# Layer 3's product jobs spread over all eight steps of a group, value banks emptied by VectorE, and layer 4's first pair of heads among layer 3's last steps

## What is computed

```python
x = _layernorm(x + _L1_attn_ref(x, Wq, Wk, Wv, Wo, lambda_init))      # layer 3: difference attention
x = _layernorm(x + _L1_xattn_ref(x, ctx_2048, ctx_2048, gamma))       # layer 4: attention over the context
x = _layernorm(x + _L1_ffn_ref(x, ...))                               # layer 5: experts
```

## Time and profile before

| | |
|---|---|
| median of 3 runs | 2112.47 us (2110.99 to 2131.47) |
| profiled execution | 2109.85 us |
| its span | 2107.8 us |
| layer 3's loop and end | about 420 to 754 us of the span |
| layer 4 up to its steady part | about 754 to 783 us |

### The profile page before, as it was taken

The page is one execution under the profiler, slowest core; times in us unless marked ns, Lnnn a source line. Parts: engine busy times, 40 slices in busy tenths (PEclk is TensorE's granted clock), DMA queues, the critical chain, the costliest instruction groups (busy, mean ns, idle before and its releaser), DMA issues.

```text
span 2107.8 us, 30014 instructions
## 1 busy us (share of the span) xinstructions
PE 1858.5 (88%) x11146; PEld 1440.5 (68%) x11160; DVE 1253.2 (59%) x2718; ACT 1014.5 (48%) x2260; POOL 618.5 (29%) x654
## 2 busy tenths in 40 slices
PE   8998898789889779789999979876999788999796
PEld 6885776667777644478888865655888644555585
DVE  3555784466666745544444454685444567888666
ACT  3124784254454447623333322663333369889232
POOL 1212100132232321112222224442222234888322
PEclk9998897899999979889999989986999898999888
DMA  5005402100010110023332310000323101000011
GB/s 211 26 26 120 72 2 93 41 1 7 35 38 1 38 38 1 1 74 123 110 107 98 127 59 1 1 10 31 118 98 102 50 1 38 1 1 1 0 61 41
DMA packets 25622, 105.57 MB, mean 50 GB/s; under 512 B 3642, under 2 KB 9530, under 8 KB 21508
## 3 DMA queue, kind: packets, MB, share of 16 engines
q1 hardware_dynamic: 23316, 101.87, 14.2%
q0 software_dynamic: 1728, 1.58, 0.7%
q10 hardware_dynamic: 432, 0.20, 0.0%
HBM read 97.56 MB, written 6.07 MB: 49 GB/s over the span
## 4 chain that ended last, share of the span: by engine, by line
PE 67%; DVE 14%; ACT 9%; issue 4%; POOL 3%; DMA 2%; SPq 0%; POOLq 0%; DVEq 0%; ACTq 0%
PE ps L145 60%; PE ps L262 6%; ACT AR L148 4%; DVE AR L162 3%; DVE AR L151 2%; DVE Y L151 2%; DVE AR L159 1%; POOL AR L151 1%; DVE stt L325 1%; POOL R L151 1%; DMA AR<-sq 1%; DVE X L156 1%; DVE W L159 1%; POOL rs L151 1%; ACT AR L1680 1%
## 5 line engine op out<-in xcount | busy, mean ns | idle before, releaser
L145 PE MATMUL ps<-R 128*128 128x512 f32 (+3 forms) x4944 | 879.1, 343 | 55.7 <-POOL R L151 33.1
L145 PEld LDWEIGHTS ps<-R 128*128 128x128 f32 (+1 forms) x4944 | 750.4, 194 | 171.9 <-issue 30.9
L151 POOL TENSOR_TENSOR R<-W,R 128x768 fp32r<-128x768 f32 (+2 forms) x106 | 181.5, 1724 | 600.8 <-ACT R L1934 496.0
L148 ACT ACTIVATE AR<-AR 128x128 f32<-128x128 f32 (+4 forms) x585 | 277.4, 549 | 162.0 <-DVE AR L162 106.7
L151 DVE TENSOR_TENSOR AR<-ps,AR 128x512 f32<-128x512 f32 (+5 forms) x266 | 137.5, 536 | 239.8 <-PE ps L145 220.0
L262 PEld LDWEIGHTS ps<-cf,AR 128*128 128x128 f32 (+1 forms) x1168 | 145.8, 148 | 168.2 <-issue 61.0
L262 PE MATMUL ps<-cf,AR 128*128 128x128 f32 (+1 forms) x1168 | 193.6, 290 | 53.2 <-POOL AR L151 14.0
L1960 ACT CAST R<-AR 128x512 fp32r<-128x512 f32 x148 | 92.0, 622 | 304.1 <-DVE AR L151 294.4
L145 PE MATMUL ps<-W,AR 128*128 128x256 f32 (+3 forms) x1200 | 212.3, 353 | 22.1 <-ACT AR L1370 12.5
L145 PE MATMUL ps<-AR 128*32 128x256 f32 (+4 forms) x1600 | 188.0, 337 | 10.3 <-DVE AR L151 7.6
L145 PEld LDWEIGHTS ps<-W,AR 128*128 128x128 f32 (+2 forms) x1200 | 156.9, 164 | 55.0 <-issue 20.5
(11 more groups left out here) (186 smaller groups left out, 2048.2 us busy)
## 6 DMA issues: line engine op xcount, KB each, us to landing
W<-in_wts SPq DMA_DIRECT2D x14, 1920.0 KB, 7.9
AR<-shd SPq DMA_DIRECT2D x32, 512.0 KB, 3.6
W<-in_wts SPq DMA_DIRECT2D x4, 2048.0 KB, 8.5
AR<-shd SPq DMA_DIRECT2D x20, 384.0 KB, 3.4
W<-in_wts SPq DMA_DIRECT2D x5, 1280.0 KB, 7.5
AR<-shd SPq DMA_DIRECT2D x20, 256.0 KB, 3.9
W<-in_wts SPq DMA_DIRECT2D x2, 1536.0 KB, 7.7
AR<-shd SPq DMA_DIRECT2D x20, 128.0 KB, 3.7
```

Source lines behind the costliest of these rows:

```text
L145: return self.e.matmul(o, l, r, start=start, stop=stop, skip_group_check=True)
L148: return self.e.activation(o, i, f, bias=bias, scale=scale)
L151: return self.e.tensor_tensor(o, a, b, op)
```

## The change

In layer 3 the 12 product jobs of the next group are dealt out over all eight steps: 1, 2, 2, 2, 2, 1, 1, 1 jobs in the steps b = 0 to 7. The q and k parts of the weights are split two groups ahead, in step b = 5 of the group before, and the v part in step b = 0. The v banks are copied by DVE. The transposed state is no longer made. Layer 4's first pair moves into layer 3's end: POOL's part into step 60, the scores into step 66, the maxima into 68 and 69, the exponentials into 69; for that its tiles of the first pair lie in the tensor CR. Layer 4's pairs use the score banks 2, 3, 0, 1 in turn. Layer 10's mask is made in layer 5's step 6.

```diff
@@ stage counts
-                N[_l] = Ends(*stage(added=8, aggr=8, rstd=8, normed=8, xturned=8, xt=8))
+                turns = 0 if _l == 3 else 8
+                N[_l] = Ends(*stage(added=8, aggr=8, rstd=8, normed=8, xturned=turns, xt=turns))
@@ need_state_bank
+            elif l == 4:
+                e.wait_ge(*N[3].added.at(8))
@@ DifferenceAttention
-                return job[0] == "v" or (job[0] != "o" and job[2] == 1)
+                return job[0] in ("q", "k") and job[2] == 1
...
                 g, b = divmod(i, 8)
-                return self.products(g + 1)[2 * (b - 1):2 * b] if g < 7 and 1 <= b <= 6 else []
+                first = (0, 1, 3, 5, 7, 9, 10, 11, 12)
+                return self.products(g + 1)[first[b]:first[b + 1]] if g < 7 else []
...
+            @staticmethod
+            def splits(i):
+                g, b = divmod(i, 8)
+                if b == 5 and g < 6:
+                    return [(g + 2, 0), (g + 2, 1)]
+                return [(g + 1, 2)] if b == 0 and g < 7 else []
+
+            def need_split(self, e, g, i):
+                e.wait_ge(*loaded(first_chunk[self.l] + g // 2))
+                if g:
+                    e.wait_ge(*self.T.worked.at(self.place[self.products(g - 1)[7 if i < 2 else 11]] + 1))
... pe
-                    if i >= 63:
+                    if i == 66:
                         e.wait_ge(*T.biased.at(64))
-                        pe_turn_state(e, self.l, i - 63)
-                pe_turn_state(e, self.l, 7)
+                        layers[4].pe_scores(e, 0)
... dve_job
+                    if job[0] == "v":
+                        _, g, t0 = job
+                        e.e.tensor_copy(self.v[g % 2][:, 256 * t0:256 * (t0 + 2)], k).then_inc(T.taken_d.sem, 1)
+                        return
... dve
+                layers[4].dve_parity(e)
...
+                    if i >= 68:
+                        layers[4].dve_max(e, i - 68)
... act
+                for i in range(2):
+                    self.act_split(e, 1, i)
                 for i in range(70):
...
-                        if i % 8 == 0 and i < 56:
-                            self.act_split(e, i // 8 + 1)
+                        for g, part in self.splits(i):
+                            self.act_split(e, g, part)
                     for job in self.jobs(i):
                         self.act_job(e, job)
-                    if i >= 63:
-                        act_copy_state(e, self.l, i - 63)
-                act_copy_state(e, self.l, 7)
+                    if i == 69:
+                        layers[4].act_exps(e, 0)
... pool (the subtractions follow splits(i) in the same way)
+                    if i == 60:
+                        layers[4].pool_front(e)
@@ ColumnAttention
+                early = Room((CR[:, 512:4608].bitcast(F32), 2048), (CR[:, 7168:10368].bitcast(F32), 1600))
+                self.E, self.OS = early.ring(4, 512), room.ring(2, 512)
+                self.KB = [early.take(512), room.take(512)]
+                self.VZ = [early.take(512), room.take(512)]
+                self.OZ, self.par = early.take(64), early.take(2)
+                self.m = early.ring(4, 4)
...
+            def score_bank(i):
+                return banks[(i + 2) % 4]
...
+            def pool_front(self, e):
+                T = self.T
+                e.wait_ge(s_y, 32)
+                e.wait_ge(*T.parity.at(1))
+                self.pool_keys(e, 0)
+                e.e.memset(self.VZ[0], 0.0).then_inc(T.zeroed.sem, 1)
+                e.e.memset(self.OZ, 0.0).then_inc(T.zeroed.sem, 1)
+                e.wait_ge(*T.zeroed.at(2))
+                for h in range(2):
+                    e.e.memset(self.OZ[:, 48 * h:48 * h + 16], 1.0).then_inc(T.ones.sem, 1)
+                e.wait_ge(*T.ones.at(2))
+                self.pool_values(e, 0)
@@ LargeAndSmallExperts, dve_route
+                if j == 6:
+                    layers[10].dve_mask(e)
@@ vector engine
-                    if layer is layers[4]:
-                        layers[10].dve_mask(e)
```

More of the change, by code:

```diff
@@ L1334, in dve, with act_split @@
                     dve_norm(e, self.l, b)
[L1336 to L1342 removed]
+            def act_split(self, e, g, i):
+                self.need_split(e, g, i)
+                e.e.copy(self.part(self.WH, i), self.parts(g)[i]).then_inc(self.T.wh.sem, 1)
             def act_job(self, e, job):
@@ L1407, in pool @@
                              ALU.mult).then_inc(T.scaled.sem, 1)
-                    if i % 8 == 0 and i < 56:
-                        split(i // 8 + 1)
+                    for g, part in self.splits(i):
+                        split(g, part)
+                    if i == 60:
+                        layers[4].pool_front(e)
                     if i >= 62:
@@ L1608, in pe @@
                 for v in range(42):
[L1609 to L1618 removed]
+                    if 0 < v < 32:
+                        self.pe_scores(e, v)
                     if 1 <= v <= 32:
@@ L1634, in dve @@
                 need_room(e, l)
-                e.red(self.par, cfc("bm16").rearrange("p (n h) -> p h n", h=2), ALU.add).then_inc(T.parity.sem, 1)
-                for i in range(83):
+                for i in range(2, 83):
                     if i < 64:
-                        e.wait_ge(*T.scored.at(i // 2 + 1))
-                        e.wait_ge(*T.exped.at(i - 3))
-                        e.red(self.m[i % 4][:, 0:2], banks[i % 4].rearrange("p (h w) -> p h w", h=2), ALU.max,
-                              negate=True).then_inc(T.maxed.sem, 1)
+                        self.dve_max(e, i)
                     b, r = divmod(i - 18, 8)
@@ L1660, in dve_end, with act_exps @@
                     dve_add(e, self.l, b, OS[:, 256:512])
+            def act_exps(self, e, v):
+                T = self.T
+                for i in (2 * v, 2 * v + 1):
+                    e.wait_ge(*T.maxed.at(i + 1))
+                    e.wait_ge(*T.turned.at(i // 2 - 1))
+                    for h in range(2):
+                        s = slice(256 * h, 256 * (h + 1))
+                        t = e.act(self.E[i % 4][:, s], self.score_bank(i)[:, s], ACT.Exp, bias=self.m[i % 4][:, h:h + 1])
+                    t.then_inc(T.exped.sem, 1)
             def act(self, e):
@@ L1664, in act @@
                 for v in range(42):
-                    if v < 32:
-                        for i in (2 * v, 2 * v + 1):
-                            e.wait_ge(*T.maxed.at(i + 1))
-                            e.wait_ge(*T.turned.at(i // 2 - 1))
-                            for h in range(2):
-                                s = slice(256 * h, 256 * (h + 1))
-                                t = e.act(self.E[i % 4][:, s], banks[i % 4][:, s], ACT.Exp, bias=self.m[i % 4][:, h:h + 1])
-                            t.then_inc(T.exped.sem, 1)
+                    if 0 < v < 32:
+                        self.act_exps(e, v)
                     if 1 <= v <= 32:
```

115 lines of the change are left out of this document (54 added, 61 removed).

## The result

The changed kernel takes 0.9928 of the time before, with a 95% interval of 0.9902 to 0.9954: 15.2 us less on 2112 (9.7 to 20.7). The ratio is that of the means of 20 runs each; their medians, 2103.67 and 2114.31 us, lie 10.6 apart. The forecast was 35.6 less. The profiled execution took 2095.47 us, its span is 2093.4.

What follows compares the result with a forecast made beforehand. PE and its two shared banks bound the loop, a chain of norms and transposes the layer's end; 6.9 + 6.5 + 9.5 + 9.3 + 3.7 - 0.3 = 35.6 off 2112.5 gave 2077, 8-in-10 range 2063 to 2091.

Steps and rivals of the forecast that it cites:

- The loop: Layer 3's groups: period from 41.14 to 40.3 us, six times, plus 1.6 for a slow job pair; 6.9 us gained.
- a late multiplication of POOL's: Layer 3, step b = 5: probabilities' multiplication 0.7 us late behind two subtractions, 0.3 of it left at b = 1.
- the lock: Layer 3's join on DVE, locked out behind a POOL subtraction: up to 1.3 us later, sum 6 us worse; not priced in.
- a period above 41: Sign of being wrong: a group of layer 3's loop taking above 41 us, where 40.3 was forecast.
- a clock at 0.50: Sign of being wrong: PE's granted clock at 0.50 anywhere between 420 and 760 us.
- Group 0: Layer 3's first group, before its first "o": q's first job starts at once, 6.5 us gained.
- Layer 3's end: Without the turned state DVE leads, last norm at 744.1 instead of 753.58: 9.5 us gained.
- Layer 4's front: Third pair's exponentials come 3.7 us after layer 3's last norm instead of 13.0: 9.3 us gained.
- The clock there: Layer 4's first rounds run at full clock, since no PE gap exceeds 2 us from 724 us on: 3.7 gained.
- rival 1: Layer 4 still starts at the slow clock, without the 3.7 us and perhaps one slow round more: 2081; chance 0.25.
- The mask: Layer 5: 2.6 us of DVE work hidden behind a full PE, at most 0.3 us lost.
- Rival 2: Layer 3's loop: no "o" waits for ACT, PE's 35.9 us a group, 26 us less: 2051; chance 0.1.

Runs made afterwards that it cites:

- the scalar form: Changed kernel with DVE's 128x2 lambda multiplication written as two 128x1 multiplications by a scalar: ratio 0.9904 in every pass, 0.9896 in pass b = 1 only.
- the mask in step 40: Changed kernel with layer 10's mask made in step 40 of layer 5 in place of step 6: ratio 0.9926.
- the swap: Changed kernel with ACT emptying the h = 0 q/k banks and DVE the h = 1 banks, instead of the reverse: ratio 0.9765.

## Why the prediction was wrong

The forecast was 35.6, measured are 15.2 (9.7 to 20.7). Its range ended at 2091 and the median is 2104.

- **The loop, 6.9: the step that failed.** It gave nothing (+2.5 in this pair of traces). The wait for ACT was forecast and came: "o" waits for ACT's copy in steps b = 1 to 4, 6.16 us a step, v steps at 3.8. The term failed on b = 1, priced at 6.05 and measured at 7.48. Of the 1.43, 0.96 is DVE's multiplication held beside POOL's subtraction (0.8 of it taken away by experiment), and 0.38 DVE's copy in front of the add, which is read from the timeline and not tested ("PE hides it, with 0.2 us to spare": on average it did, but it left the add late where the loop closes). The 0.3 a group for a late multiplication of POOL's doesn't show: the other four steps took 3.91, 3.80, 3.80 and 3.75, where 3.83, 3.94, 3.94 and 3.79 were priced. So a group came out 0.9 over 40.3, 5.5 in six. I had weighed the lock and dismissed it for POOL's even durations. They could not show it: it was DVE that came second. And I looked for it at the join, not at the smallest instruction of the pass. With the lock at "six times some 1 us", which stood in the text as what the rule of the Trainium skill would make of it, this term would have been about 1. The Trainium skill's page "SBUF — State Buffer", "Who interferes with whom", states that such a pair locks out whichever comes second for the whole instruction; the trace agrees (0.16 to 1.12 us, ending with POOL's), and so does the scalar form, which has one SBUF tensor and wasn't held. The first group also kept two slow steps (7.96 and 8.04 us) where I took the slow pair as gone: 43.55 us (453.51 to 497.06), 2.3 over the period. The clock has most of that: it was granted at 0.50 from 465 to 469 us, and in the trace of the same loop without this dip (the mask in step 40) the second of these steps takes 6.15. A second dip, in the next group, is the 1.1 of its b = 2. The sign of being wrong that was set down, a period above 41, came, and so did the one of a clock at 0.50.
- **Group 0, 6.5.** Right: 6.8.
- **Layer 3's end, 9.5.** Right mechanism, 8.1. PE had a part in it again: it ran at the slow clock from about 734.2 to 737.7, behind a gap of 1.95. The last norm came 15.5 us after the first one, where 14 was forecast.
- **Layer 4's front, 9.3.** Right: 9.1 in all, third pair 3.6 after the norm.
- **The clock there, 3.7.** It did not come; rival 1 did, at its price. "No PE gap over 2 us" was a wrong test: from 724 us on the longest gap was 1.95, and 1.58 at the handover, and the clock fell behind a stretch busy 2.01 of 4.00, although one busy 2.27 of 4.00 had stayed at full clock before. Filled with idle work, the handover gave 4.5.
- **The mask, -0.3.** Not contradicted as far as layers 4 and 5 go (-0.6; but this stretch takes 454.4 to 459.4 over all traces, so a term of 0.3 can't be read there). That unchanged layers behind could take 6.1 back was in no case of mine.
- **Rival 2** had the right arithmetic: PE's own sum of 35.9 a group is 36.2 once no "o" waits for ACT and the lock is gone, and its 26 us were there for one line: the swap alone takes 26.5 off steps 8 to 56 of the kernel before.

Misses of 9.4, 1.4, 3.9 and 6.1, less 1.2 where it gave more, make 19.6 of the 20.4 between forecast and measurement. That they close so well is luck: the interval of the timed runs is 11 us wide, and single stretches such as the loop differ by 2 to 3 us between traces of the same code.

## What to carry to other kernels

Where two engines empty a pair of shared banks, give the bank that is reused first to the engine that is done first, not to the one behind the long work; here that was worth 30 us and the rest of the loop's rewrite 6. A VectorE instruction with two SBUF inputs that starts behind a GpSimd instruction ends with it, however small it is itself (0.16 us became 1.12): look at the tiny ones when such work is moved, and write them in scalar form in just the passes that collide and lie on the path. And keep TensorE fed over a handover between stages, before the clock has fallen rather than after.

## What the runs showed of the hardware

A 128x2 multiplication on DVE took 1.12 us instead of 0.16 when it started 0.2 us behind a subtraction on POOL, and 0.16 where it was over before one began; POOL's own durations didn't change (median 1.30 us in both kernels). TensorE stayed at a granted clock of 0.50 from 755 to 763 us though it was busy for all of it, and 22 products around the handover kept it at 1.00; the same number behind a gap of 3.58 us brought it back after some 7 us instead of 23 and gained no time. The Trainium skill ("TensorE: Matmul & The Clock Gate", "What's actually happening") states that activity releases the clock; these traces agree for the handover and for the products behind the gap. By themselves the 8.00 of 8.00 us that the profile counts as busy did not release it, and there the traces do not bear that sentence out. Layers 6 and 7 took 180.3 us in both traces of the kernel before and 182.9 to 187.8 in every kernel with the new end, and 190.5 in one whose only edit lies over 300 us ahead of them: a gain of a few microseconds in one layer can't be read from the time of such a program.
